# Adding expert outputs to the token rows in memory instead of in a closing stage

## The reference, cut to what matters

```python
h = h + attention(layernorm(h))                     # the "h1" rows below
xf = layernorm(h).reshape(-1, D)                    # 10880 x 128
gate_vals, idx = top_k(xf @ router_w, 2)
gates = softmax(gate_vals)
out = 0
for e in range(8):
    y = layernorm_e(xf + relu(xf @ w1[e] + b1[e]) @ w2[e] + b2[e])   # F = 512
    out = out + sum(where(idx == e, gates, 0))[:, None] * y
return h + out
```

## Time and profile before

| | us |
|---|---|
| median of three runs | 1102.32 (1100.51 to 1102.33) |
| the profiled execution's own time | 1104.65 |
| its span, first to last instruction | 1102.9 |
| TensorE busy in the span | 880.8 (80%) |
| VectorE busy | 789.5 (72%) |
| GpSimd busy | 445.1 (40%) |
| first load of an expert tile issued | 701.06 |
| closing stage, first load issued | 1059.32 |

### The profile page before, as it was taken

The page is one execution under the profiler, slowest core; times in us unless marked ns, Lnnn a source line. Parts: engine busy times, 40 slices in busy tenths (PEclk is TensorE's granted clock), DMA queues, the critical chain, the costliest instruction groups (busy, mean ns, idle before and its releaser), DMA issues.

```text
span 1102.9 us, 27762 instructions
## 1 busy us (share of the span) xinstructions
PE 880.8 (80%) x7792; PEld 730.5 (66%) x7793; DVE 789.5 (72%) x3172; ACT 554.0 (50%) x1512; POOL 445.1 (40%) x491
## 2 busy tenths in 40 slices
PE   1577888879899999988989973499999999899900
PEld 1467888865676666666667652388888888888800
DVE  1488887754766666667776655189999998899956
ACT  0212111006867666677787642266666666566600
POOL 3000000000144444444554445267777777777720
PEclk9989888898867777789997765699999999999955
DMA  7363441015011111111111111632222222222259
GB/s 132 62 94 51 67 65 23 1 57 165 24 37 43 40 40 40 39 42 50 45 46 47 42 45 40 204 137 75 67 71 70 72 69 66 70 70 73 61 210 397
DMA packets 69073, 84.09 MB, mean 76 GB/s; under 512 B 12051, under 2 KB 53702, under 8 KB 68858
## 3 DMA queue, kind: packets, MB, share of 16 engines
q1 hardware_dynamic: 54282, 54.93, 20.2%
q0 software_dynamic: 12256, 22.50, 6.6%
q10 hardware_dynamic: 2448, 5.57, 1.3%
HBM read 48.15 MB, written 35.71 MB: 76 GB/s over the span
## 4 chain that ended last, share of the span: by engine, by line
PE 52%; issue 14%; DVE 13%; ACT 8%; DMA 5%; another core or an unknown queue 3%; SPq 2%; DVEq 1%; POOL 1%; ACTq 0%; POOLq 0%
PE ps L650 7%; PE ps L885 6%; DVE arena L986 4%; PE ps L706 4%; PE ps L876 4%; PE ps L874 3%; PE ps L731 3%; DMA arena<-y_tokens 3%; PE ps L717 3%; PE ps L875 3%; PE ps L799 2%; PE ps L712 2%; PE ps L766 2%; PE ps L785 2%
## 5 line engine op out<-in xcount | busy, mean ns | idle before, releaser
L552 POOL DMA_INDIRECT x_slots<-arena x192 | 184.2, 959 | 264.2 <-DVE arena L1191 66.5
L579 POOL DMA_INDIRECT y_tokens<-arena x184 | 184.7, 1004 | 46.2 <-issue 43.8
L1538 ACT ACTIVATE arena<-ps,b_t 128x256 f32<-128x256 f32 x368 | 156.8, 478 | 88.3 <-PE ps L876 80.2
L885 PE MATMUL ps<-arena 128*128 x1472 | 181.0, 276 | 0.0
L885 PEld LDWEIGHTS ps<-arena 128*128 128x128 f32 x1472 | 171.6, 192 | 1.9
L650 PE MATMUL ps<-wt,arena 128*128 128x128 f32 x960 | 131.0, 299 | 8.7 <-DVE h L1008 8.7
L650 PEld LDWEIGHTS ps<-wt,arena 128*128 128x128 f32 x960 | 125.6, 213 | 10.2 <-DVE arena L986 10.2
L874 PE MATMUL ps<-arena 128*128 128x256 f16 x368 | 101.5, 276 | 21.2 <-DVE arena L1263 12.4
L1401 ACT ACTIVATE arena<-ps 128x340 f32<-128x340 f32 (+3 forms) x160 | 70.0, 447 | 65.8 <-PE ps L793 24.2
L876 PE MATMUL ps<-arena 128*128 128x256 f16 x368 | 100.9, 274 | 0.0
L875 PE MATMUL ps<-arena 128*128 128x256 f16 x368 | 100.9, 274 | 0.0
(11 more groups left out here) (203 smaller groups left out, 1844.4 us busy)
## 6 DMA issues: line engine op xcount, KB each, us to landing
arena<-x_slots SPq DMA_DIRECT2D x92, 130.0 KB
arena<-y_tokens SPq DMA_DIRECT2D x17, 640.0 KB, 14.8
h<-h_rows SPq DMA_DIRECT2D x1, 5440.0 KB
out<-h ACTq DMA_DIRECT2D x17, 320.0 KB, 9.5
arena<-x_in SPq DMA_DIRECT2D x64, 84.5 KB
arena<-x_in SPq DMA_DIRECT2D x64, 78.0 KB
h_rows<-h SPq DMA_DIRECT2D x32, 128.0 KB
x_slots<-arena POOLq DMA_INDIRECT x192
```

The costliest lines, as they stand in the source:

```text
L552: pool.indirect_dma_start(xs_dram, bass.IndirectOffsetOnAxis(ap=slot_i[n][0:rows, t, k:k + 1], axis=0), row[n][0:rows, k, t, :], None).the ...
L579: pool.indirect_dma_start(y_dram, bass.IndirectOffsetOnAxis(ap=y_id[n % 2][:, k:k + 1], axis=0), y_sl[n % 2][:, k, :], None, bounds_check= ...
L885: ins = pe.matmul(ps[6 + m][:, 128 * k:128 * k + 128], hid[m][:, c, 128 * k:128 * k + 128], w2_sb[:, bass.ds(e, 1), c, :].rearrange("p o n ...
L1538: act.activation(hid[m][:, c, :], ps[2 + 2 * m + c // 2][:, SLOT * (c % 2):SLOT * (c % 2) + SLOT], ACT.Relu, bias=b1_t[:, bass.ds(e * FC + ...
```

## The change

- `y_dram` and `h1_dram` are dropped. SyncE stores the h1 rows straight into the output, which gets 256 more rows that are cut off on the host.
- GpSimd's `scatter_y` now adds (`compute_op=ALU.add`) the rows to the output row of their token. Both copies of a token carry the same id t. There is no bounds check: pad rows carry ids 10880 to 11135, the additional rows.
- Two tiles of different experts may hold the same token, and an add reads its row before it writes it. So the first tile of an expert, and every tile behind the last used one, waits until the rows of the tile before it have landed. Which tiles these are is known only from the counts: VectorE works out a third table, `gone_tab`, of semaphore values, with four more small instructions and one more copy, TensorE makes a third transpose, and GpSimd reads one value of it into a register for each tile.
- GpSimd zeroes the additional rows ahead of the attention scatters (two DMAs), and ahead of the expert stage it waits for these and for all stored h1 rows.
- The reload of the h1 rows (L435) and the closing stage are gone. At its end GpSimd waits until all adds have landed.
- `shifted` waits as before, with counts that are 16 higher.

```diff
@@ scatter_y, GpSimd
             def scatter_y(i, n, u, e):
+                gone = pool.value_load(gone_tab[0:1, bass.ds(i, 1)], min_val=16, max_val=16 + 32 * (NTILE // YBUF))
                 pool.wait_ge(S["y_ready"], i + 1)
+                pool.wait_ge(y_gone[(n - 1) % YBUF], gone)
                 apart(pool)
                 for k in range(2):
                     pool.indirect_dma_start(
-                        y_dram, bass.IndirectOffsetOnAxis(ap=y_id[n % 2][:, k:k + 1], axis=0),
-                        y_sl[n % 2][:, k, :], None, bounds_check=2 * NTOK - 1, oob_is_err=False,
-                    ).then_inc(y_gone[n % 2], 16)
+                        out_rows, bass.IndirectOffsetOnAxis(ap=y_id[n % 2][:, k:k + 1], axis=0),
+                        y_sl[n % 2][:, k, :], None, compute_op=ALU.add,
+                    ).then_inc(y_gone[n % YBUF], 16)
@@ ahead of and behind the tiles, GpSimd
             pool.wait_ge(S["tab_ready"], 1)
+            pool.wait_ge(S["h1_stored"], 32 * PAIRS)
+            for gone in y_gone:
+                pool.wait_ge(gone, 16)
             tiles(pool, Chain(pool, None), 0, 0, tile_iteration)
+            for gone in y_gone:
+                pool.wait_ge(gone, 16 + 32 * (NTILE // YBUF))
@@ the table, VectorE (gone[:, 0] is 32 but for tile 0; gone[:, 1] is 16 + 32 * ((tile - 1) // 2), at least 16)
+            ch.link(dve.tensor_scalar(first[:, 0:NEXP - 1], tile_end[:, 0:NEXP - 1], tile_no, None, ALU.is_equal))
+            ch.link(dve.tensor_scalar(first[:, last], tile_end[:, last], tile_no, None, ALU.is_le))
+            ch.link(dve.tensor_reduce(tab_f[:, 2:3], first, AX_X, ALU.max))
+            ch.link(dve.scalar_tensor_tensor(tab_f[:, 2:3], tab_f[:, 2:3], con("gone")[:, 0:1], con("gone")[:, 1:2], ALU.mult, ALU.add))
...
+            ch.link(dve.tensor_copy(gone_tab[:, :], ps[1][0:1, 256:256 + XBUF * NBLOCK]))
@@ closing stage, SyncE, VectorE, ScalarE
-            sp.wait_ge(S["h1_stored"], 32 * PAIRS)
-            sp.dma_start(h1_rows, h1_dram.rearrange("(p j) n -> p (j n)", p=128)).then_inc(S["h1_loaded"], 16)
...
-            for gone in y_gone:
-                sp.wait_ge(gone, 32 * (NTILE // 2))
-                sp.dma_start(y_tok[c % YBUF], y_part[:, SUM_ROWS * c:SUM_ROWS * c + SUM_ROWS]).then_inc(y_loaded[c % YBUF], 16)
-                    dve.tensor_tensor(rows, rows, y_tok[c % YBUF][:, :, k, :], ALU.add).then_inc(S["sum_ready"], 1)
-                act.dma_start(out_part[:, part], h1_rows[:, part]).then_inc(S["h_out"], 16)
@@ GpSimd, ahead of the attention scatters
-            pool.memset(pad_row[:, :, 129:130], float(PAD_ID)).then_inc(S["pad_ready"], 1)
+            pool.wait_ge(S["pad_ready"], 2)
+            for m in range(YBUF):
+                pool.dma_start(out_rows[NTOK + 128 * m:NTOK + 128 * m + 128, :], pad_row[:, m, 0:E_DIM]).then_inc(y_gone[m], 16)
```

More of the change, by code:

```diff
@@ L62, in const_layout @@
         ("eo", 2), ("meanv", 128), ("before", 128), ("reset", TOK),
-        ("cls_sel", PCOLS), ("expert", 8), ("region", 8), ("eps", 8), ("tokid", PTILES), ("slotid", 2),
+        ("cls_sel", PCOLS), ("expert", 8), ("region", 8), ("eps", 8), ("tokid", PTILES), ("slotid", 2), ("gone", 2),
         ("tiles_k", 43), ("one_row", 128),
@@ L102, in const_array @@
     put("eps")[:, 6] = 1 / 16
-    put("tokid")[:] = 2 * (r[:, None] + 128 * np.arange(PTILES)[None, :])
+    put("tokid")[:] = r[:, None] + 128 * np.arange(PTILES)[None, :]
     put("slotid")[:] = np.arange(128)[:, None] + 128 * np.arange(2)[None, :]
+    put("gone")[:, 0] = 32 * (r > 0)
+    put("gone")[:, 1] = np.maximum(16 + 32 * ((r - 1) // YBUF), 16)
     put("tiles_k")[:] = SLOT * np.arange(43)
@@ L272, in build @@
         more, ntiles, tile_end, skip = A1.take(NEXP, 43), A1.take(NEXP), A1.take(NEXP), A1.take(NEXP)
-        past, skipped, tab_f = A1.take(NEXP), A1.take(NEXP), A1.take(2)
+        past, skipped, first, tab_f = A1.take(NEXP), A1.take(NEXP), A1.take(NEXP), A1.take(3)
         assert A1.at <= PHASE1_WORDS, A1.at
@@ L297, in build @@
         y_id = [A3.take(2, dt=I32) for _ in range(2)]
-        y_tok = [A3.take(SUM_ROWS, 2, E_DIM) for _ in range(YBUF)]
-        h1_rows = h[:, :, :, :].rearrange("p a c n -> p (a c n)")[:, 0:PART_ROWS * E_DIM]
         assert A3.at <= PHASE1_WORDS
         tile_tab = sb("tile_tab", [1, XBUF * NBLOCK], I32)
+        gone_tab = sb("gone_tab", [1, XBUF * NBLOCK], I32)
         expert_tab = sb("expert_tab", [1, NBLOCK, 2 * XBUF], I32)
@@ L1182, in gates @@
                 ch.step(dve.reciprocal(row[p % ROWS][:, 0, :, 128], den[:, :]))
-                dve.tensor_scalar(row[p % ROWS][:, 1, :, 129], ids[:, :], 1.0, None, ALU.add).then_inc(S["gate_done"], 1)
+                dve.tensor_copy(row[p % ROWS][:, 1, :, 129], ids[:, :]).then_inc(S["gate_done"], 1)
             def place(p, par):
@@ L1189, in place @@
                 ch.step(dve.tensor_tensor(row[p % ROWS][:, 1, :, 128], row[p % ROWS][:, 0, :, 128], edif[:, :], ALU.mult))
-                ch.link(dve.tensor_scalar(ids[:, :], ids[:, :], float(2 * PT), None, ALU.add))
+                ch.link(dve.tensor_scalar(ids[:, :], ids[:, :], float(PT), None, ALU.add))
                 dve.tensor_copy(slot_i[p % ROWS][:], slot_f[:]).then_inc(S["slots_ready"], 1)
@@ L1587 @@
         aps[name] = nc.dram_tensor(name + "_in", arr.shape, DT.from_np(arr.dtype), kind="ExternalInput").ap()
-    out = nc.dram_tensor("out", (NTOK, E_DIM), F32, kind="ExternalOutput").ap()
+    out = nc.dram_tensor("out", (OUT_ROWS, E_DIM), F32, kind="ExternalOutput").ap()
     build(nc, aps, out)
     r = run_bass_kernel_spmd(nc, [arrays], core_ids=[0])
-    return r.results[0]["out"].reshape(BATCH, TOK, E_DIM)
+    return r.results[0]["out"][:NTOK].reshape(BATCH, TOK, E_DIM)
```

41 lines of the change are left out of this document (12 added, 29 removed).

## The result

| | before | after |
|---|---|---|
| median, us | 1102.32 | 1153.23 (1147.39 to 1158.51, 4 runs) |
| ratio after to before | | 1.047, 95% interval 1.038 to 1.055 |
| span of the profiled execution | 1102.9 | 1146.5 |
| first load of an expert tile to the end | 401.8 | 458.4 |
| GpSimd busy | 445.1 (40%) | 563.0 (49%) |

The account below looks back on a forecast made before the run. Bounds: TensorE, closely followed by VectorE, in the tiles, and memory bandwidth in the closing stage. Terms: -43.2 + 1.15 + 9.2 + 3 + 2 - 0.5 = -28.4 us from 1102.32, rounded 1074 us; range 1061 to 1130.

Parts of the forecast that it names:

- the descriptor work of an add: GpSimd's indirect DMA in each tile: the rows' part doubles, +0.07 us for each DMA, and the rest stays fixed.
- L': Time from an adding DMA's end until its rows land: 2.3 us taken against 1.15 now, +1.15 us once at the end.
- Rival A: GpSimd's indirect DMA in every tile: generating adds makes GpSimd the bound, slower from d = 1.34 us an instruction; chance 0.16.
- the doubling: GpSimd's descriptor generation doubles for adds: its cycle becomes 5.4 us and the kernel some 140 us slower.
- The closing stage: End of the kernel, after SyncE's wait for the last y rows: 43.6 us, its removal gains 43.2 us.
- the pad tiles: Tiles 88 to 91 at the end each wait for the tile before to land: 4 x 2.3 = +9.2 us.
- The waits at experts' ends: First tiles of seven experts wait for the tile before to land: 7 x 0.4, say +3 us.
- The register load: GpSimd loads one register for each tile: 0.15 us taken, nothing at best, 0.3 to 0.5 us at worst.
- rival B: Loop over the two y buffers: late landings make it the bound, passing 3.69 us from L' = 2.7 on; chance 0.17.
- The start: Start of the expert stage: without the h1 reload tiles load sooner, -0.5 us (-1.9 to 0).

Follow-up runs that it names:

- the last two kernels with adds: Changed kernel with b2 on TensorE (f32, then f16), pad rows dropped, no pad-tile waits, SyncE waiting for the last adds: 1150.76 us, then 1098.12 us.
- the kernel with b2 in f16: Changed kernel with b2 added on TensorE by f16 matmuls, pad rows dropped, no pad-tile waits, SyncE waiting for the last adds: 1098.12 us.

## Why the prediction was wrong, point by point

**The step that failed** is the descriptor work of an add: "I take the slope: the rows' part twice, +0.07 us for each DMA." It was +0.57 us (1.57 against 1.00), eight times as much. Both of its halves were wrong: a row costs about four times what it did, not twice (2.3 against 0.6 ns at most), and the part that the slope called fixed is fixed for a plain write only; an add brings 0.4 us of its own. The slope of the plain write said nothing about the fixed part of the add. The upper bound of 2.0 us, if all of it doubled, did hold it. The prediction named L', the landing, as its weakest point; it broke at the length of the instruction.

**Rival A was the case.** The runs with plain writes, in which only `compute_op` goes, show it. It put the border at d = 1.34 us. Its formula with the measured 1.57 gives a cycle of 3.2 + 0.15 + 1.14 = 4.49 us, against 4.56 and 4.50 measured from transposes to transposes, and 1071.9 + 88 x 0.80 = 1142 us. In part the nearness is luck: the steady cycle is 4.45, without a register load to speak of and with some first DMAs of 1.8 us, and the measured means hold the longer waits at experts' ends. The chance of 0.16 for it, of which 0.10 on the slower side, was too small for a price that no row bounded from above by less than 2.0, with a break-even a third above the base: the middle of that interval, 1.5, was already on the losing side. The measured 1153 also lies above the range, whose end at 1130 stood for d = 1.5. The Trainium skill (Collectives: The Full Stack, The bandwidth ceiling), by which an add in the DMA engines needs two source reads, pointed the right way, to a dearer instruction: the runs show 1.6 times the duration, between the row's 1.07 and the doubling. The prediction's 140 us for the doubling is not what its own formula gives: 1071.9 + 88 x 1.66 is 1218 us, 116 slower.

**The closing stage** was priced right as to what it frees: it took 43.6 us and is gone. But from the start of the last DMA to the end only 38.6 us were won, 3.5 less than predicted: the 0.4 us behind the last landing became GpSimd's drain of 3.4 us, as GpSimd now works last. Giving the wait to SyncE, as in the last two kernels with adds, left 5.9 us from the start of the last DMA to the end against 7.1 to 7.2, a gain of 1.2 us only; GpSimd's drain record is there still, 8.4 us long, from among its last DMAs to the end.

**The landing of an add** was taken as 2.3 us; at the end it was at most 1.8 (1140.88 to 1142.7). The gaps of 2.5 to 3.2 us in the pad tiles hold 0.7 us and more beyond that, which the prediction left out. Of these 0.3 stand between any two DMAs; what fills the rest is not shown. With plain writes it is the same 0.7 us (a gap of 2.05, and at the end at most 1.33 from 1048.07 to 1049.4). The two errors cancel: 11.0 us in four gaps, less the 1.2 that stood there, are +9.8 against +9.2 predicted. The remaining 7.5 us of that stretch fit the longer instructions of its 13 last DMAs (13 x 0.57 = 7.4). The estimate from the Trainium skill's times for an access to memory (DMA: Bandwidth & Descriptors, Latency and other measured facts) put the landing between 1.35 and 3.15; the trace's 1.8 at most lies in the lower part of it.

**The waits at experts' ends** were +3 us in the sum, since GpSimd's slack was to take up the rest; it had none left. They show as seven steps of 6.2 to 6.8 us in place of 4.45, 13.8 us together. They bind only where GpSimd is the bound: with plain writes, and in the kernel with b2 in f16, the pace of TensorE hides most of them.

**The register load** costs nothing, as one bound had it: 0.17 us stand between bias add and DMA, where 0.15 stood. **The two-buffer loop** (rival B) was not the bound, although its sign, VectorE waiting for landed rows in nearly every tile, is in the trace. The third buffer showed that here the wait is a symptom. **The start** was to gain 0.5 us. The first of the tiles' DMAs started 19.9 to 20.0 us after the first load in the three profiles of the kernel before, 23.2 and 20.7 in the two of the kernel after; whether this reached the end is not shown.

**Open.** On the chip where the kernel before takes 997 us, the kernel with plain writes gained 0.7% only, 5 us, with a stretch of 371.4 us. No profile of the kernel before was taken there, so it isn't shown where the other 20 us were.

## What to carry to other kernels

Before work is moved onto a queue that has half a microsecond to spare in each round, price the new instruction by itself: a form of it that the trace does not show may have another fixed cost, and the base case should then lie in the middle of the bounds, not at the end that the nearest row suggests. Divide the whole gain by the number of rounds first: here 30 us over 88 tiles were 0.35 us a tile, so, with the 0.5 us that GpSimd had to spare, the entire case hung on two instructions growing by no more than about a third of a microsecond each. And when an engine waits for a landing in every round, ask who starts the transfers late; more buffers did not help behind a queue that was too slow.

## What the runs showed of the hardware

- An indirect DMA that adds kept GpSimd busy for 1.57 us (128 rows) and 1.42 us (64 rows); one that writes took 0.95 to 1.0 us for 128 rows.
- An add lands little later than a write: the gap that a wait for landed rows leaves on GpSimd was mostly 2.5 us after adds (up to 3.2), mostly 2.05 us after plain writes (up to 2.4).
- GpSimd's queue drained at the end of the program though all rows had landed: for 3.4 us after adds of 128 rows (3.7 with three buffers), 5.4 us after adds of 64 rows, 5.9 us after plain writes. On what it depends was not tried.
- VectorE's norm (L1294 before, L1295 after) took 531 ns on average in the kernel before, 700 and 634 in the two profiles with adds, and 667 and 605 with plain writes, so the adds are not its cause. Without the bias add on GpSimd it took 359. The two meet at the bias add; what they share was not tried.
- The first of a tile's two DMAs took now 1.57, now 1.80 us in the kernel after. Without the bias add on GpSimd it was 1.55 us in the median, and still up to 1.79.
